# VectorE's norm and routing pieces placed between the sine products and the cosine product of the queries, in a transformer layer with forgetting attention and a mixture of experts

## What is computed

```python
# attention: 16 heads of 128; keys and values are one shared head, scaled per head
q = (x @ Wq.T).reshape(b, n, H, D);  kv = x @ Wkv.T;  kv_head = x @ Wkvh.T
kv_head = cumsum(kv_head * exp(cumsum(log_sigmoid(x @ Wg.T))))   # shifted by one token
k, v = kp[..., None, :] * kh[..., None], vp[..., None, :] * vh[..., None]
q, k = rope(q), rope(k)                                        # cosine and sine products
p = softmax(where(mask, q @ k.T / sqrt(D), -inf))
out = (p @ v).reshape(b, n, H * D) @ Wout.T
# moe: 8 experts, 2 per token, 640 slots each, and one shared MLP
top, sel = top_k(x @ router, 2);  weights = softmax(top)
y = sum over the chosen experts of weights * down(silu(gate) * up)  + shared_mlp(x)
```

## Time and profile before

| | |
|---|---|
| three runs, median | 791.88 us (791.78, 791.88, 792.73) |
| profiled execution, its own time | 792.51 us |
| its span | 790.5 us |
| TensorE busy | 739.8 us (94%) |
| VectorE busy | 574.6 us (73%) |
| ScalarE busy | 467.8 us (59%) |
| GpSimd busy | 544.3 us (69%) |
| mean granted TensorE clock | 0.991 |
| the 64 steps of the loop | from about 50 to 560 us |

### The profile page before, as it was taken

How to read it: one execution, slowest core, us unless ns; L and a number is a source line. 1 busy time by engine, 2 the same in 40 slices (tenths; PEclk the granted TensorE clock), 3 DMA queues, 4 the chain that set the end, 5 groups by cost and what they waited for, 6 DMA issues and landing times.

```text
span 790.5 us, 14041 instructions
## 1 busy us (share of the span) xinstructions
PE 739.8 (94%) x4364; PEld 628.5 (80%) x4364; DVE 574.6 (73%) x1539; ACT 467.8 (59%) x1163; POOL 544.3 (69%) x459
## 2 busy tenths in 40 slices
PE   5799999999999999999999999999899989899993
PEld 4587788888888888888777888777778879888882
DVE  6976886777777766868887777988754447777577
ACT  5567776676666676765666766665633246554262
POOL 4466998787878887777888888778534253431773
PEclk9999999999999999999999999999999999999997
DMA  9411245422222212222222221212142035441352
GB/s 299 124 53 54 84 158 180 156 72 72 63 68 66 74 61 69 62 67 58 65 65 83 82 80 61 63 58 64 48 152 71 34 139 199 176 166 67 88 149 84
DMA packets 47748, 75.73 MB, mean 96 GB/s; under 512 B 9728, under 2 KB 24640, under 8 KB 47680
## 3 DMA queue, kind: packets, MB, share of 16 engines
q1 hardware_dynamic: 43504, 65.19, 26.6%
q0 software_dynamic: 3072, 8.39, 3.4%
q10 hardware_dynamic: 1104, 1.31, 0.5%
HBM read 57.71 MB, written 17.17 MB: 95 GB/s over the span
## 4 chain that ended last, share of the span: by engine, by line
PE 71%; DVE 11%; issue 8%; ACT 4%; POOL 3%; DMA 2%; DVEq 0%; ACTq 0%; POOLq 0%
PE ps L433 20%; PE ps L969 16%; PE ps L934 13%; PE ps L985 9%; PE ps L955 7%; PE ps L1133 3%; POOL got L1883 1%; DVE q_sw L1315 1%; DVE q_sw L1314 1%; DVE hid_both L1646 1%; POOL slot_inputs L1790 1%; DVE hid_hi L1636 1%; POOL o_lo L1774 1%; DVE hid L1641 1%; DVE hid L1633 1%
## 5 line engine op out<-in xcount | busy, mean ns | idle before, releaser
L969 PE MATMUL ps<-pt,vp 128*128 128x512 f32 (+3 forms) x512 | 149.5, 434 | 10.3 <-DVE q_sw L1315 10.0
L634 ACT ACTIVATE prob<-ps,neg_max 128x512 f32<-128x512 f32 (+3 forms) x256 | 132.6, 525 | 34.7 <-DVE neg_max L1324 30.6
L969 PEld LDWEIGHTS ps<-pt,vp 128*128 128x128 f32 x512 | 82.7, 190 | 59.9 <-issue 30.5
L1324 DVE CUSTOM_DVE_ANT_0 ps<-ps,causal_row 128x512 f32<-128x512 f32 (+3 forms) x256 | 120.1, 511 | 5.5 <-PE ps L934 5.4
L1755 POOL TENSOR_TENSOR q_sw<-q_cos,q_sw 128x512 f32<-128x512 f32 x62 | 79.2, 1277 | 64.4 <-DVE q_cos L1316 64.3
L643 ACT ACTIVATE pt<-ps,vcol 128x512 f32<-128x512 f32 x64 | 44.1, 690 | 109.5 <-PE ps L955 109.5
L1774 POOL TENSOR_TENSOR o_lo<-o_t,o_hi 128x512 fp32r<-128x512 f32 x64 | 84.3, 1317 | 33.4 <-ACT o_hi L672 33.4
L955 PE MATMUL ps<-id_f,prob 128*128 128x128 f32 x640 | 92.3, 275 | 0.9 <-ACT pt L643 0.9
L934 PE MATMUL ps<-k_hi,q_hi 128*128 128x512 f32 x248 | 87.1, 351 | 0.4 <-POOL q_lo L1759 0.3
L1759 POOL TENSOR_TENSOR q_lo<-q_sw,q_hi 128x512 fp32r<-128x512 f32 x62 | 80.2, 1293 | 4.0 <-ACT q_hi L666 3.6
L1343 DVE TENSOR_TENSOR o_t<-ps,inv_row 128x512 f32<-128x512 f32 x64 | 44.3, 692 | 52.5 <-PE ps L969 52.5
(11 more groups left out here) (220 smaller groups left out, 1940.2 us busy)
## 6 DMA issues: line engine op xcount, KB each, us to landing
kh_row<-kvh_rows SPq DMA_DIRECT2D x64, 256.0 KB, 3.2
inv_row<-inverse_sums SPq DMA_DIRECT2D x64, 256.0 KB, 3.2
slot_inputs<-zeros SPq DMA_DIRECT2D x8, 640.0 KB, 4.9
xg<-slot_inputs SPq DMA_DIRECT2D x8, 640.0 KB, 4.5
slot_outputs<-yo SPq DMA_DIRECT2D x8, 640.0 KB, 3.3
up_raw<-in_w_up_dram SPq DMA_DIRECT2D x8, 368.0 KB, 4.8
wo_raw<-in_wout_dram SPq DMA_DIRECT2D x4, 512.0 KB, 7.9
dn_sb<-in_w_dn_dram SPq DMA_DIRECT2D x8, 256.0 KB, 3.7
```

The costliest lines, as they stand in the source:

```text
L634: ins = act.activation(prob[:, i % 2, ROW_AT[nt]:ROW_AT[nt] + w], ps_s[bank][:, at:at + w], ACT.Exp, scale=-1.0, bias=neg_max[:, i % 2, nt ...
L969: ins = pe.matmul(ps_qo[:, mt * P:SEQ], vp[:, b * TPB + mt, :], pt[:, i % 2, cols], start=(mt == 0), stop=(mt == PT_BANKS[-1][-1]))
L1324: ins = dve.tensor_tensor_reduce(s_, s_, causal_row[:, (NT - 1 - nt) * P:], 1.0, BIG, ALU.add, ALU.min, neg_max[:, i % 2, nt:nt + 1])
```

## The change

In the step of VectorE's program, `rope_products` is cut in two. The sine products are made right after `inverses` and `rest_of_wo`, then come the norm and routing pieces, then the cosine product. Before the loop `rope_products` stays as it was. No instruction is added or taken away, and no semaphore is changed.

```diff
-            def rope_products(i):
+            def sine_products(i):
                 dve.wait_ge(q_psum, i + 1)
                 if i:
                     dve.wait_ge(q_ready, i)
                 dve.tensor_tensor(q_sw[0:64, :], ps_qo[64:P, :], sin_sb[64:P, :], ALU.mult)
                 dve.tensor_tensor(q_sw[64:P, :], ps_qo[0:64, :], sin_sb[0:64, :], ALU.mult).then_inc(q_sin_ready, 1)
+
+            def cosine_product(i):
                 dve.tensor_tensor(q_cos[:], ps_qo[:], cos_sb, ALU.mult).then_inc(q_cos_ready, 1)
+
+            def rope_products(i):
+                sine_products(i)
+                cosine_product(i)
...
                 if i + 1 < UNITS:
                     inverses(i + 1)
+                if i > 1 and wo_head(i - 2) is not None:
+                    rest_of_wo(wo_head(i - 2))
+                if i + 3 < UNITS:
+                    sine_products(i + 3)
                 for b in range(B - 1):
                     n = i - back_step(b)
...
                     elif n == POSITIONS + 1:
                         find_slots(b)
-                if i > 1 and wo_head(i - 2) is not None:
-                    rest_of_wo(wo_head(i - 2))
                 if i + 3 < UNITS:
-                    rope_products(i + 3)
+                    cosine_product(i + 3)
                 if i == 0:
                     rope_products_of_keys(B - 1)
```

## The result

| | before | changed |
|---|---|---|
| six runs each, median | 792.17 us (791.78 to 792.92) | 797.58 us (795.95 to 799.12) |
| profiled execution, its own time | 792.51 us | 796.45 us |
| its span | 790.5 us | 794.5 us |

The changed kernel is slower by 0.66%: the ratio of its runs to those of before is 1.0066, 95% interval 1.0051 to 1.0081. That is 5.4 us; 6 were forecast on a median of 791.88. (Slips ahead of the prediction: norm pieces stand at n = i - 17, i - 33 and i - 49, not at i - 17 (b + 1); the routing pieces of the second batch at n = i - 46, not i - 47; and the loop's last division starts at 578.4 us, not before 560. The steps that the prediction names are right.)

What follows compares the result with a forecast made beforehand. TensorE, busy 94% of the span, was taken to bound the kernel. New stalls of 10.6 us, less 5.2 given back, plus 0.8 for longer products, gave +6.2, taken as +6: 797.9 us, range 794.0 to 801.3.

Steps and rivals of the forecast that it cites:

- The deadline: Ahead of `weigh_values`: TensorE waits for VectorE's cosine product, which can be 0.57 us late for nothing.
- The exposed pieces: 13 steps from 17 to 57: pieces no longer hidden in VectorE's 1.69 us wait for queries; 10.6 us of new stalls.
- The released holds: Steps 38, 40, 42, 44, 54, 56, 58, 60: stalls fall from 10.5 to 5.3 us, 5.2 given back.
- The cost of a stall on the next product: TensorE's product after each stall takes 0.07 us longer; eleven more stalls, 0.8 us.
- The hold: A small SBUF-to-SBUF operation of VectorE is held while GpSimd has a row of work; 3.46 us in step 42.
- Rivals 1 and 2: 1: release outweighs exposure, result 789, chance 0.08. 2: the two cancel, within 1.6 us of now, chance 0.05.
- Rival 3: Steps 38 to 44 and 54 to 60: GpSimd's row follows the late cosine, 3 to 5 us on top; chance 0.08.
- Rival 4: Steps 42, 44, 58, 60: hold not tied to GpSimd's row, so stalls stay; +10.5 us, chance 0.04.
- Rival 5: TensorE's clock: more stalls might bring one or two half-rate stretches of 1.7 us each; +9, chance 0.02.
- What I said would show it: `weigh_values` waits for VectorE 18 times, 13 us; statistics steps 8.8 to 8.9 us; 3.46 us addition under 1 us.
- step 3: Ninth of today's `weigh_values` stalls, 0.8 us, from the gates; forecast to stay.

Runs made afterwards that it cites:

- e6: Changed kernel with 1 to 6 extra VectorE statistics between sine and cosine products in steps 10 to 15; 802.07 us, 4.5 over the changed kernel's median.
- e5: All pieces moved behind the cosine product, sine and cosine products together, against the kernel before; 809.44 us against 791.98.
- e2: Changed order in all steps but 38, 40, 42, 44, 54, 56, 58 and 60, against the kernel before; 806.96 us against 792.11.
- e1: Changed order only in steps 38, 40, 42, 44, 54, 56, 58 and 60, against the kernel before; 785.87 us against 792.11.
- e8: Kernel before with one extra small VectorE operation behind inverses in steps 23, 39, 45 to 48 and 55; 804.08 us in one run (792.96 before).
- e3: Kernel before with GpSimd waiting ahead of scale_keys in steps 42, 44, 58 and 60 for VectorE's small operation; 788.08 us against 792.11.
- e9: The kernel of e2 run once more, unchanged; 805.09 us in the one run, 12.1 above the kernel before.
- e7: Changed kernel with 7 extra VectorE statistics between sine and cosine products in each of steps 10 to 15; 808.07 us.

## Why the prediction was right

**The deadline** (the cosine, 0.57 us of it free) is shown: the start of `weigh_values` follows the cosine by 0.10 in every step in which it stalls itself, e6 gives the threshold between one statistic and two and the full price beyond it, and e5 takes this wait away by taking the pieces out of the cosine's way, though others come in its place.

**The exposed pieces** were forecast at 10.6 + 0.9 = 11.5 us for 13 steps and measured at 11.3 with steps 20 and 23. Off by 0.1 or more are 33, 34, 49 and 50 (0.10 to 0.12 too high), 39 and 55 (0.2 too high: the hold of the normalisation was 0.5, not 0.8), and 20 and 23, which I had at nothing: a normalisation that GpSimd's last instruction holds reaches past the 0.57. e2 shows the losses alone, and that they do not depend on the gains.

**The released holds** were forecast at 5.4 and measured at 5.9; e1 shows them alone, 6.6 in the trace. The term that was mis-sized is the variances of 42 and 58: 0.5 and 0.4 of stall were left by the forecast, 0.39 and 0.22 in the trace. The loop came out 0.7 under the sum, as both the losses and the gains erred to that side. **The cost of a stall on the next product**, 0.07, is in it too and came out as read.

**The hold** was named rightly (GpSimd's row) and its rule wrongly. I took it that a small operation waits for a gap in GpSimd's work, always. Steps 39 and 23 of the kernel before already had normalisations that got in at the first hand-over. e8 gives the rule for this kernel: to the first hand-over as a rule, to the first gap where an indirect DMA was issued ahead of the row. The forecast did not suffer, since behind the sines only GpSimd's last instruction is left to hold anything; the expectation of e5 did. What the Trainium skill says in "SBUF — State Buffer", "Who interferes with whom", the other is blocked until the instruction ends, is what step 39 of e8 shows (1.24 us), and not what step 45 shows (3.72 us).

**Rivals 1 and 2** fell by e1 and e2: the exposure is twice the release. **Rival 3** (GpSimd's row follows) is seen at 0.39 us in steps 38, 42, 54 and 58 of e2, 1.6 us in all where I priced it at 3 to 5. In the changed kernel itself it is the 0.42 and 0.29 us by which steps 42 and 58 are longer than in e1. **Rival 4** fell by e3 and e1: a gap ends the hold, and behind the sines it is gone. **Rival 5**, the clock, I gave 0.02. The changed kernel's profiled execution has no fall in steps 1 to 60, but e2, e5 and e8 have. The changed kernel's six runs spread over 3.2 us, those of before beside them over 1.1 and nine others of before over 2.3. The mean granted clocks of the six, 0.990 to 0.993, lie within what the kernel before shows, 0.989 to 0.993: falls as many as in e5 (0.98) are not in them. A single fall would not stand out there, and only one of the six has a trace; whether some had one stays open.

**What I said would show it** held for the step lengths, the 3.46 us addition and the sines' wait. It failed for the list of waits: I expected 18 waits for VectorE and 13 us, and it shows 12 under "issue" and 9.1 us, 13 and 9.9 with step 3.

## What to carry to other kernels

Before moving work to where it looks cheaper, ask which idle time hides it now: pieces that cost nothing while VectorE waited for the queries cost their full length less 0.57 us once they stood between the two products. Look at each step on its own: the same edit lost 11 us in one set of steps and won 6 in the other. Where a small operation is long only because it is held by another engine's work, let that engine wait for it, if it has time to spare, rather than move the small one; here this won 11.2 us.

## What the runs showed of the hardware that I had not expected

- An indirect DMA issued by GpSimd changes how long VectorE is held afterwards: a 128x4 addition that starts during the first of three GpSimd `tensor_tensor` instructions is released after 1.05 to 1.26 us without it, and after 3.70 to 3.72 us, behind all three, with it; a wait of GpSimd that makes a gap releases it (2.22 us, e3). Why the DMA does this is not shown.
- TensorE's granted clock fell to half for 3.4 us at a time inside the loop of three kernels, each time next to the end of an idle time of TensorE: four of 2.80 to 3.05 us in e5, all of them with a fall, one of 1.76 in e2 and one of 1.72 in e8. Idle times of 1.76 and 1.71 in e9 and 1.71 in e8 brought none, nor did six of 1.55 or 1.56 in a row, one in each step of 9.75 us (e7). What tells the cases near 1.7 apart was not tried.
- The idle time that the profile shows ahead of a group of matmuls, and the engine that it names, are poor counters of stalls: 10.0 us before and 9.9 after, while the stalls' cost went from 11.1 to 16.5 us by step lengths (step 3 left out of these two). Starts of instructions are exact; they, and not the ends, are to be compared.
